# Routed gated layer on one core: turns without work passed at once, two homes for the raw weights, first weights loaded among the tiles

## The reference

```python
# first layer: a sigmoid of an outer sum, mixed with the layer norm of x
xij = sigmoid(si[:, :, None] + sj[:, None, :] + b[0])     # si, sj: ctx times two weight vectors
x = x + tanh(g_xattn[0]) * (0.6 * xij + 0.4 * layernorm(x))
# second layer: every token goes to one expert
xt = layernorm(x).reshape(-1, 1024)
probs = softmax(xt @ wg);  idx = argmax(probs);  gate = probs[idx]
out = gate * (xt @ W[idx].T + b[idx])
x = x + tanh(g_ffn[0]) * out
```

## Time and profile before

| | us |
|---|---|
| median of 3 runs | 708.17 |
| lowest, highest | 706.31, 712.63 |
| the profiled execution | 711.4 |
| its span, first to last instruction | 709.7 |
| matmuls of the slot loop, first to last | 236.3 to 661.8 |

### The profile page before, as it was taken

The page is one execution under the profiler, slowest core; times in us unless marked ns, Lnnn a source line. Parts: engine busy times, 40 slices in busy tenths (PEclk is TensorE's granted clock), DMA queues, the critical chain, the costliest instruction groups (busy, mean ns, idle before and its releaser), DMA issues.

```text
span 709.7 us, 15153 instructions
## 1 busy us (share of the span) xinstructions
PE 576.9 (81%) x2841; PEld 459.3 (65%) x2842; DVE 425.7 (60%) x559; ACT 272.5 (38%) x408; POOL 331.2 (47%) x489
## 2 busy tenths in 40 slices
PE   7898888867480699997899998899999799899300
PEld 5576666645260588786688887687788688788200
DVE  3276777867637576766777577757674677544000
ACT  2385776646430343433434333433333343322000
POOL 1466777764422344453454544444544454366300
PEclk8598999987885799999899999899999999999755
DMA  7942576573535678786797688867786777555200
GB/s 268 377 97 75 195 239 228 192 235 94 180 120 197 165 203 248 192 243 196 199 254 210 189 219 247 210 189 225 214 213 189 222 217 209 171 170 185 68 5 4
DMA packets 84562, 134.06 MB, mean 189 GB/s; under 512 B 9856, under 2 KB 66176, under 8 KB 84480
## 3 DMA queue, kind: packets, MB, share of 16 engines
q1 hardware_dynamic: 74688, 99.46, 50.8%
q0 software_dynamic: 9792, 33.82, 12.3%
HBM read 99.44 MB, written 35.91 MB: 191 GB/s over the span
## 4 chain that ended last, share of the span: by engine, by line
SPq 26%; issue 20%; PE 17%; DMA 15%; DVE 9%; ACT 4%; POOL 2%; DVEq 1%; ACTq 0%; POOLq 0%
PE pair L942 6%; DMA w_raw<-in_L_ffn_W 5%; SPq L278 5%; SPq L314 5%; PE pair L931 4%; DMA rows<-table 4%; DMA out_x<-rows,scatter_row 3%; SPq L338 3%; PE pair L915 3%; SPq L353 2%; PE pair L920 2%; SPq L357 2%; DVE xr L699 2%; SPq L354 2%; DVE pair L740 2%
## 5 line engine op out<-in xcount | busy, mean ns | idle before, releaser
L1004 PE MATMUL pair<-wt,xt 128*128 x1728 | 405.5, 397 | 40.1 <-DVE xt L785 20.1
L1004 PEld LDWEIGHTS pair<-wt,xt 128*128 128x128 f32 x1728 | 329.3, 191 | 115.9 <-issue 43.7
L740 DVE STREAM_TRANSPOSE pair<-w_raw 128x1024 f32<-128x1024 f32 x64 | 80.6, 1259 | 75.4 <-DMA w_raw<-in_L_ffn_W 72.3
L578 ACT ACTIVATE wt<-pair 128x1024 f32 (+1 forms) x64 | 65.7, 1027 | 145.6 <-DVE pair L740 145.6
L491 POOL TENSOR_TENSOR rows<-rows,rb 128x1024 f32<-128x1024 f32 x37 | 89.1, 2407 | 69.6 <-ACT rb L622 69.6
L745 DVE TENSOR_TENSOR wt<-pair,wt 128x1024 f32 (+1 forms) x64 | 77.5, 1211 | 12.5 <-ACT wt L578 12.5
L942 PE MATMUL pair<-xc_tr,wg_sb 128*8 128x128 f32 x512 | 73.6, 307 | 0.0
L622 ACT ACTIVATE rb<-bias_bc,scal 128x1024 f32 (+1 forms) x37 | 46.0, 1244 | 71.3 <-POOL scal L488 59.2
L609 ACT ACTIVATE xt<-pair 128x1024 fp32r<-128x1024 f32 x38 | 38.9, 1025 | 67.9 <-DVE pair L781 67.8
L781 DVE STREAM_TRANSPOSE pair<-xb 128x1024 f32<-128x1024 f32 x38 | 47.9, 1260 | 25.0 <-DMA xb<-table 21.5
L942 PEld LDWEIGHTS pair<-xc_tr,wg_sb 128*8 128x8 f32 x512 | 48.7, 100 | 18.6 <-issue 3.3
(11 more groups left out here) (125 smaller groups left out, 426.9 us busy)
## 6 DMA issues: line engine op xcount, KB each, us to landing
w_raw<-in_L_ffn_W SPq DMA_DIRECT2D x128, 256.0 KB
xb<-table SPq DMA_DIRECT2D x156, 128.0 KB, 3.3
rows<-table SPq DMA_DIRECT2D x38, 520.0 KB, 4.8
xr<-in_x SPq DMA_DIRECT2D x32, 512.0 KB, 7.5
ctx_in<-in_ctx SPq DMA_DIRECT2D x8, 512.0 KB, 5.6
bias_bc<-in_L_ffn_b SPq DMA_DIRECT2D x28, 128.0 KB, 2.9
out_x<-rows,scatter_row POOLq DMA_INDIRECT x36, 5.0
bias_bc<-in_L_ffn_b SPq DMA_DIRECT2D x1, 512.0 KB, 18.3
```

What stands on the lines that cost most here:

```text
L578: nc.scalar.activation(wt[:, bass.ds(par, 1), 0, :, bass.ds(j * (P * PG) + P * n, P)].rearrange("p a k o -> p (a k) o"), ps[:, :].rearrang ...
L740: nc.vector.transpose(turned(ps), blocked(w_raw[:, n, :, :])).then_inc(w_turned, 1)
L1004: last = nc.tensor.matmul(out_ps[r % 2][:, HALF * h:HALF * (h + 1)], xt[:, r % RING, x_part, k, :], wt[:, bass.ds(par, 1), w_part, k, HALF ...
```

## The change

The kind in `slot_tab` now has only 0, 1 and 2 (with a granule). `w_raw` has two homes; a slot's granule lies in the home of the slot's parity. SP, in slot t, reads the kind of slot t + 1 and, if that has weights, loads its granule: it reads its row in `W` and, from a new sixth row of the table, the count of pieces that must be turned first (those of all granules up to slot t - 1's), and also waits until all earlier granules have landed. On every engine each turn of six slots now stands inside an `If` on the kind of its first slot. `load_first(0)` and `load_first(1)` stand behind the loads of tiles 18 and 20, `load_first(2)` to `(4)` behind the last tile load, each needing only the granule two before it to be turned. The planner makes the new row.

```diff
-        w_raw = sb("w_raw", [P, PG, NB, QW])
+        w_raw = sb("w_raw", [P, 2, PG, NB, QW])
...
-            def load_granule(row0):
+            def load_granule(row0, home):
                 for q in (0, 2, 1, 3):
-                    sp.dma_start(w_raw[32 * q:32 * (q + 1), :, :, :].rearrange("p m b c -> p (m b) c"),
+                    sp.dma_start(w_raw[32 * q:32 * (q + 1), home, :, :, :].rearrange("p m b c -> p (m b) c"),
                                  in_blocks(W_rows[row0, :], q, PG * NB)).then_inc(w_landed, 16)
             def load_first(g):
                 if g:
-                    sp.wait_ge(w_turned, PG * g)
-                load_granule(slice(P * PG * g, P * PG * (g + 1)))
-            load_first(0)
+                    sp.wait_ge(w_landed, 64 * g)
+                if g > 1:
+                    sp.wait_ge(w_turned, PG * (g - 1))
+                load_granule(slice(P * PG * g, P * PG * (g + 1)), g % 2)
...
             for t in range(RX, T):
                 sp.wait_ge(row_stored[slot_of(t)], 16)
                 sp.dma_start(xr[:, slot_of(t), 0:H], tile_of(x_t, t)).then_inc(x_landed[slot_of(t)], 16)
-            for g in range(1, GRAN + 1):
+                if t in (RX + 2, RX + 4):
+                    load_first((t - RX) // 2 - 1)
+            for g in range(2, GRAN + 1):
                 load_first(g)
...
             with slot_loop(sp) as i:
-                for r in range(TURN):
-                    t = TURN * i + r
-                    work = sp.value_load(slot_tab[0:1, 0, bass.ds(t, 1)], min_val=0, max_val=3)
+                begun = sp.value_load(slot_tab[0:1, 0, bass.ds(TURN * i, 1)], min_val=0, max_val=2)
+                with sp.If(begun > 0):
+                    for r in range(TURN):
+                        t = TURN * i + r
+                        work = sp.value_load(slot_tab[0:1, 0, bass.ds(t, 1)], min_val=0, max_val=2)
...
-                            with sp.If(work > 2):
-                                o = sp.value_load(slot_tab[0:1, 4, bass.ds(t, 1)], min_val=0, max_val=E * H - P * PG)
-                                settled(w_turned, K * e + K + PG * j + PG)
-                                load_granule(bass.ds(o, P * PG))
+                            ahead = sp.value_load(slot_tab[0:1, 0, bass.ds(t + 1, 1)], min_val=0, max_val=2)
+                            with sp.If(ahead > 1):
+                                o = sp.value_load(slot_tab[0:1, 4, bass.ds(t + 1, 1)], min_val=0, max_val=E * H - P * PG)
+                                g = sp.value_load(slot_tab[0:1, 5, bass.ds(t + 1, 1)], min_val=1, max_val=E * K)
+                                settled(w_turned, g)
+                                settled(w_landed, o // (P * PG // 64))
+                                load_granule(bass.ds(o, P * PG), (r + 1) % 2)
...
-                nc.vector.transpose(turned(ps), blocked(w_raw[:, n, :, :])).then_inc(w_turned, 1)
+                nc.vector.transpose(turned(ps), blocked(w_raw[:, home, n, :, :])).then_inc(w_turned, 1)
...
-            nc.vector.tensor_scalar(with_load[:, :], granule[:, :], float(GRAN * E - 1), 1.0, ALU.is_lt, ALU.add)
-            link(nc.vector.tensor_scalar(granule[:, :], granule[:, :], 1.0, float(P * PG), ALU.add, ALU.mult))
-            link(nc.vector.tensor_tensor(kinds[:, :], not_last[:, :], with_load[:, :], ALU.mult))
-            nc.vector.tensor_scalar(slot_tab[:, 4, :], granule[:, :], float(E * H - P * PG), None, ALU.min)
+            link(nc.vector.tensor_tensor(kinds[:, :], not_last[:, :], used[:, :], ALU.mult))
+            nc.vector.tensor_scalar(slot_tab[:, 4, :], granule[:, :], float(P * PG), float(E * H - P * PG), ALU.mult, ALU.min)
+            nc.vector.memset(slot_tab[:, 5, 0:1], 1)
+            link(nc.vector.tensor_tensor(before_it[:, 1:TAB], granule[:, 1:TAB], kinds[:, 0:TAB - 1], ALU.subtract))
+            nc.vector.tensor_scalar(slot_tab[:, 5, 1:TAB], before_it[:, 1:TAB], float(PG), float(E * K), ALU.mult, ALU.min)
```

More of the change, by code:

```diff
@@ L145, in build @@
         n_begun, newest, nth, base, not_last = [spare[0][:, TAB * j:TAB * (j + 1)] for j in range(5)]
-        used, kinds, granule, with_load = [spare[1][:, TAB * j:TAB * (j + 1)] for j in range(4)]
+        used, kinds, granule, before_it = [spare[1][:, TAB * j:TAB * (j + 1)] for j in range(4)]
         wt = sb("wt", [P, 2, 2, K, H], F32R)
@@ L496, in _ @@
             with slot_loop(pool) as i:
[L497 to L509, removed]
+                begun = pool.value_load(slot_tab[0:1, 0, bass.ds(TURN * i, 1)], min_val=0, max_val=2)
+                with pool.If(begun > 0):
+                    for r in range(TURN):
+                        t = TURN * i + r
+                        work = pool.value_load(slot_tab[0:1, 0, bass.ds(t, 1)], min_val=0, max_val=2)
+                        with pool.If(work > 0):
+                            slot_scalars(t + 1, 2 * i + (r + 1) // RING, (r + 1) % RING)
+                            settled(finished, t + 3)
+                            nc.gpsimd.indirect_dma_start(
+                                out=out_rows,
+                                out_offset=bass.IndirectOffsetOnAxis(ap=scatter_row[:, r % RING:r % RING + 1], axis=0),
+                                in_=rows[:, r % RING, 0:H], in_offset=None,
+                                bounds_check=N - 1, oob_is_err=False).then_inc(out_stored[r % RING], 16)
+                        with pool.Else():
+                            pool.nop()
+                with pool.Else():
+                    pool.nop()
             held = [pool.value_load(in_place[0:1, s:s + 1], min_val=1, max_val=SLOTS) for s in range(RING)]
@@ L631, in _ @@
             with slot_loop(act) as i:
[L632 to L644, removed]
+                begun = act.value_load(slot_tab[0:1, 0, bass.ds(TURN * i, 1)], min_val=0, max_val=2)
@@ L645, in _ @@
                         with act.Else():
                             act.nop()
[L647 to L651, removed]
+                with act.Else():
+                    act.nop()
         @block.vector
@@ L867, in _ @@
             with slot_loop(dve) as i:
[L868 to L885, removed]
+                begun = dve.value_load(slot_tab[0:1, 0, bass.ds(TURN * i, 1)], min_val=0, max_val=2)
@@ new lines, in _ @@
+                with dve.If(begun > 0):
+                    for r in range(TURN):
+                        t = TURN * i + r
+                        work = dve.value_load(slot_tab[0:1, 0, bass.ds(t, 1)], min_val=0, max_val=2)
+                        home = (r + 2) % RING
+                        with dve.If(work > 0):
+                            dve.wait_ge(xt_ready, t + 2)
+                            turn_rows(t + 2, TURN // 2 * i + (r + 2) // 2, r % 2, cut_a)
+                            with dve.If(work > 1):
+                                e = dve.value_load(slot_tab[0:1, 1, bass.ds(t, 1)], min_val=0, max_val=E - 2)
+                                j = dve.value_load(slot_tab[0:1, 3, bass.ds(t, 1)], min_val=0, max_val=GRAN - 1)
+                                par = dve.snap((e + 1) % 2)
+                                turn_weights(e + 1, j, 0, r % 2, cut_b)
+                                xt_low(t + 2, home, cut_a)
+                                dve.wait_ge(xt_ready, t + 3)
+                                turn_weights(e + 1, j, 1, r % 2, cut_a)
+                                cut_low(e + 1, j, 0, par, cut_b)
+                                cut_low(e + 1, j, 1, par, cut_a)
+                                settled(w_ready, K * e + K + PG * j + PG)
+                            with dve.Else():
+                                xt_low(t + 2, home, cut_a)
+                            finish(t, r)
@@ L886, in _ @@
                         with dve.Else():
-                            xt_low(t + 2, home, cut_a)
-                        finish(t, r)
-                    with dve.Else():
-                        dve.nop()
+                            dve.nop()
+                with dve.Else():
+                    dve.nop()
         @block.tensor
```

93 lines of the change are left out of this document (58 added, 35 removed).

## The result

| | before | after |
|---|---|---|
| median of 17 runs each, us | 710.59 | 714.91 |
| lowest, highest | 703.42, 716.26 | 712.47, 719.04 |
| span of the profiled execution | 709.7 | 710.9 |
| matmuls of the slot loop, first to last | 236.3 to 661.8 | 221.6 to 693.7 |
| last matmul to end of span | 47.9 | 17.2 |

The ratio of the times is 1.0085, with a 95% interval of 1.0056 to 1.0114. It is that of the means of the fast runs, 715.38 / 709.34: the chip also has a slower state, and two of the 17 runs before, 715.16 and 716.26 us, fell in it. So the kernel after is slower by a little, inside the 1% that a measurement of this kernel can hardly tell from no change. The forecast was 728 us. A balance of near zero hides three large terms. Between the two profiles the slot loop got 46.6 us longer, the end 30.7 us shorter and the first stage 14.7 us shorter: 709.7 + 46.6 - 30.7 - 14.7 = 710.9.

The account below looks back on a forecast made before the run. SP's instruction stream was taken to set the pace of slots with weights. From the profiled span 709.7, loop +44, end -16 and first stage -8 gave 729.7; with the median 1.5 us below the span, 728 us, range 708 to 745.

Parts of the forecast that it names:

- The bound of the loop: Slot loop: SP's instruction stream sets the pace of slots with weights, about 12.8 us against PE's 11.0.
- the second home brings nothing in this kernel: Slot loop: the second home of `w_raw` relaxes only a wait that was never felt; worth 0.
- The loop's +44 us: Slot loop: 41.5 us later for the last granule plus 2.5 us of half clock; bounds +12 and +65.
- 6.6 + 3.6 - 4.7 + 2.5 = 8: Slot loop: inner slots without weights 6.6, reads of `begun` 3.6, SP slack taken up 4.7, half clock after a stall 2.5 us.
- A stall of 8 us or more at each start of an expert: Slot loop, sign to look for: PE stalls 8 us or more at each start of an expert.
- The empty turns: End of the kernel: five empty turns and the first jump back take SP 32 us against 48.7; -16 us, bounds -28 and -4.
- 0.7 + 2.4 + 0.2 + 2.8 = 6.1 us: SP's empty turn: read with branch 0.7, long forward jump 2.4, loop counter and branch 0.2, jump back 2.8 us.
- The other engines then end before SP: End of the kernel: after the change SP is still the last engine to finish.
- The first stage: Before the slot loop: earlier granule loads remove DVE's two waits, 6.8 us, and some 1 us of half clock; -8 us.
- same: Whole kernel: a time of 701 to 715 us, C and a little of the main forecast; chance 0.12.
- slower: Whole kernel: a time above the 701 to 715 us counted as no change; chance 0.79.
- C: Rival, a draw: new reads in the slot loop partly hidden, loop +20 to +28 us, 704 to 712 us; chance 0.10.

Follow-up runs that it names:

- e3_reads: The kernel before with two more table reads, values unused, on SP in each slot that loads a granule; 734.21 us against 708.13, ratio 1.0349.
- e4_packed: The kernel after with what its two new SP reads tell packed into the word a slot reads anyway; 693.79 us against 708.13 before, ratio 0.9784.
- e6_act: The kernel after, its two new reads packed into the slot's word, with ACT instead of SP issuing the bias pieces; 644.6 us against 712.12 before, ratio 0.9073.
- e5_strict: The kernel after, new reads packed into the slot's word, with the wait of a single home; 693.6 us against 712.12 before, ratio 0.9737.
- e8_after_strict: The kernel after with only the wait changed to that of a single home, all reads kept; 720.07 us against 708.42 before, ratio 1.015.
- e1_turns: The kernel before with only the test around each turn of six slots added, on every engine; 683.14 us against 708.13, ratio 0.9618.
- e2_first: The kernel before with only granules 0 and 1 loaded early among the tiles, slot loop with one home; 695.97 us against 708.13, ratio 0.9814.
- e10_after_act: The kernel after, its new reads kept, with only the bias pieces issued by ACT instead of SP; 650.31 us against 708.42 before, ratio 0.9144.

## Why the prediction was off, step by step

**The bound of the loop: right.** SP's stream sets the pace; `e3_reads` lengthens it and nothing else and pays 26 us, `e4_packed` takes two reads away and gains 22 us of loop, and `e6_act` shortens it further and PE runs almost without gaps (idle 1.75 us in 400). That the second home brings nothing in this kernel, because the earlier trace rows shows no wait for `w_turned`, held too (`e5_strict`, `e8_after_strict`).

**The loop's +44 us: right in sum, 46.6 in the profile.** Its parts were shifted. A slot costs 1.3 us more instead of 1.5: 24 x 1.3 = 31 instead of 36. In their place came a wait that the forecast priced at nothing: SP waits for ACT before the bias issue 16 times, 14.5 us, where the earlier trace rows had 4.4, so 10 us. That the two shifts cancel so nearly is luck. And the mechanism of the sum is shown for about half of it only: `e4_packed`, without the two reads, keeps 24.3 of the 46.6 us. The rest, 46.6 - 31 - 10 = 5.6 us, stands where the forecast had 6.6 + 3.6 - 4.7 + 2.5 = 8. The forecast spoke of the bias in front of the granule's load, but didn't follow the circle: with each later granule, DVE, ACT, the bias and the next load all come later too. The loads 13.3 to 13.6 us apart (13.1 to 13.3), the stores' waits at the loop's end alone and DVE's wait growing (120 us, forecast "towards 100") came about as told; the matmuls ended at 693.7 (698). A stall of 8 us or more at each start of an expert did not come: one behind a wait for weights was 9.06, the others 3.30 to 5.38.

**The empty turns: the step that failed.** The term was -16 us (its own 32 against 48.7 gives 16.7) and it measured -30.7 (-30.6 in `e1_turns`), beyond the bound of -28. Of "0.7 + 2.4 + 0.2 + 2.8 = 6.1 us" the 2.4 for the long jump and the 2.8 for the jump back were wrong together: a turn takes 1.27 us in all, so the two jumps cost some 0.4 us beyond read and branch. The forecast took the jump back's 2.8 us from the earlier trace rows as a property of the jump, and kept it even in its lower bound. But in the kernel before, SP walks through the whole turn between two such jumps, and the earlier trace rows shows what that means: five packets of instructions a turn, so that the head is gone when SP returns. The change removes the walk, and with it the reason for the stall. Only the first jump back, after a last full turn, still stalls (4.3 us), and that one was forecast too (4.3 = 2.8 + 1.5). "The other engines then end before SP" failed with it: SP is done 9.0 us before the span's end, and POOL is the last.

The Trainium skill's "Runtime: NRT & Kernel Launch", section "Instruction fetch mechanics", says that a taken branch whose target isn't in the current two pages forces a fetch before it can go on. This case's traces agree with that as far as they reach: 1.27 us and no packet with two places, 8.3 us and five packets with three. The prediction named the rule and applied it wrongly: it took the target to be outside, without counting how many places an empty turn would touch. The account by places at hand is inferred from packets and times; no trace names what an engine holds.

**The first stage: right in size.** -8 us was forecast, the profiles' mean is -9.4, `e2_first` alone measured -12 (-8 to -19 by its interval), and both waits of the earlier trace rows are gone.

With the measured turns the prediction's own sum would have been 709.7 + 44 - 30.7 - 8 - 1.5 = 713.5 us, against 714.9. The measured time lies inside the range of 708 to 745, near its low end, but at the edge of what the forecast called "same" (701 to 715, chance 0.12) and not in "slower" (0.79). The rival that comes nearest in time, C (704 to 712), has it by another mechanism: there the reads are partly hidden and the loop grows by 20 to 28 us; it grew by 46.6, and the reads of `e3_reads` cost 0.5 to 0.6 us each.

**What the change hides.** Its turns gain 31 us and its first loads 9, and its loop gives 47 back. The version that keeps the gains is `e6_act`, 9% under the kernel before: there the second home is worth 32 us, because SP is no longer the pace.

## What to carry to other kernels

If an engine's instruction stream sets the pace, a buffer that relaxes a wait brings nothing and the instructions that manage it cost in full; look first whether the wait occurs in the trace at all, then move work off that stream (here one small DMA issue with its reads and its wait: 9%, with the instruction fetches that ended with it), and only then does the buffer pay. A stall after a jump belongs to what ran since the target was last used, not to the jump: when a change removes that run, price the jump anew. The bounds of such a term come from what the engine will do after the change, not from the rows of before.

## What the runs showed of the hardware

- A jump back at a loop's end cost SP 4.9 us when its body of six slots fetched instructions on the way, and 0.3 us in `e6_act`. In 300 to 600 us the queue of instructions moved 23 packets in the kernel before, 20 in the kernel after, 1 in `e10_after_act` and none in `e6_act`. From the kernel after to `e10_after_act` SP lost one issue with its wait, two reads and one `If` a slot; somewhere between these sizes, it seems, all of the loop's code stays at hand. How much of the 49 us between `e5_strict` and `e6_act` (693.6 and 644.6 us, on one chip) is this (five stalls of 4.1 to 5.8 us in `e5_strict`, 26 in all) and how much the shorter slots was not separated.
- A read of one number from SBUF into a register takes 0.27 us by its own record but 0.5 to 0.6 us of SP's time with the pieces around it (`e3_reads`).
- Moving one DMA issue with its two reads and its wait from SP to ACT took the kernel after from 1.0085 to 0.9144 of before (`e10_after_act`). The Trainium skill's "DMA: Bandwidth & Descriptors", section "Issuing engines are not separate DMA queues", calls the sequencer time of starting a DMA, which issuing on several engines saves, usually small beside the DMA itself. Here the issue, with its reads, its wait and the fetches that ended with it, was the largest single gain measured; the issue's share alone was not measured.
